# Splitting the first load of x over two DMA queues, centring the router's weights later, and 5 filler matmuls in place of 14

## What is computed

```python
def _smooth_quant_linear(x, w):
    amax_x = jnp.max(jnp.abs(x), axis=0)          # maximum of each column
    amax_w = jnp.max(jnp.abs(w), axis=0)
    s = jnp.sqrt(jnp.maximum(amax_x, EPS) / jnp.maximum(amax_w, EPS))
    xs, ws = x / s, w * s
    x_scale = jnp.max(jnp.abs(xs), axis=-1, keepdims=True) / QMAX
    w_scale = jnp.max(jnp.abs(ws), axis=-1, keepdims=True) / QMAX
    return round(xs / x_scale) @ round(ws / w_scale).T * x_scale * w_scale.T

h = _smooth_quant_linear(layernorm(x), w1)         # first block
x = x + _smooth_quant_linear(silu(gate(h)) * up(h), w2)

xn = layernorm(x)                                  # second block
scores = xn @ router_w                             # 512 x 8
# the two best of 8 experts for each token, weighted by a softmax over the two
x = x + sum over the two of weight * (silu(xn @ gate_e) * (xn @ up_e)) @ down_e
```

## Time and profile before

| | |
|---|---|
| median of 3 runs | 396.64 us (395.88 to 397.59) |
| the profiled execution, its own time | 398.95 us |
| its span | 397.2 us |
| PE busy | 330.9 us (83%) |
| DVE busy | 223.2 us (56%) |
| ACT busy | 206.7 us (52%) |
| POOL busy | 244.7 us (62%) |
| mean granted TensorE clock | 0.948 |

### The profile page before, as it was taken

How to read it: one execution, slowest core, us unless ns; L and a number is a source line. 1 busy time by engine, 2 the same in 40 slices (tenths; PEclk the granted TensorE clock), 3 DMA queues, 4 the chain that set the end, 5 groups by cost and what they waited for, 6 DMA issues and landing times.

```text
span 397.2 us, 6211 instructions
## 1 busy us (share of the span) xinstructions
PE 330.9 (83%) x1824; PEld 198.9 (50%) x1850; DVE 223.2 (56%) x511; ACT 206.7 (52%) x386; POOL 244.7 (62%) x271
## 2 busy tenths in 40 slices
PE   5856857858887977689889896999999999999950
PEld 3434525536665953385564453555555555545520
DVE  3575886888889958877586832333333333333310
ACT  1549838968997596128544233444444444444430
POOL 6494696889999851584471262556666676656350
PEclk9999998998999598888998999999999999999996
DMA  7772907654693417045344444556677757655542
GB/s 230 233 306 88 318 21 238 216 178 136 227 320 113 161 53 266 26 159 167 152 132 162 54 130 67 104 103 117 121 130 132 131 106 116 129 86 109 87 65 26
DMA packets 27550, 56.77 MB, mean 143 GB/s; under 512 B 2624, under 2 KB 13888, under 8 KB 25600
## 3 DMA queue, kind: packets, MB, share of 16 engines
q0 software_dynamic: 8736, 20.45, 28.4%
q1 hardware_dynamic: 18256, 35.92, 26.2%
q10 hardware_dynamic: 528, 0.02, 0.1%
HBM read 37.50 MB, written 18.87 MB: 142 GB/s over the span
## 4 chain that ended last, share of the span: by engine, by line
PE 63%; DVE 15%; POOL 10%; ACT 5%; issue 4%; DVEq 0%; ACTq 0%; POOLq 0%
PE bank_h L1299 26%; PE bank_q L1320 13%; PE bank_t L1284 5%; PE bank_q L1166 4%; DVE amax L716 4%; PE bank_q L1217 4%; DVE rmax L746 3%; POOL x L638 2%; PE bank_r L1310 2%; PE bank_h L1194 2%; PE bank_r L1255 2%; DVE xn L758 2%; DVE packed L869 2%; PE bank_t L1143 2%; PE bank_r L1175 1%
## 5 line engine op out<-in xcount | busy, mean ns | idle before, releaser
L1299 PE MATMUL bank_h<-gu_hi,xT 128*128 x312 | 105.5, 384 | 2.6 <-DVE xT L952 1.9
L952 DVE SCALAR_TENSOR_TENSOR xT<-bank_t,xT 128x512 f16<-128x512 f32 x39 | 26.8, 689 | 55.1 <-ACT xT L1082 44.4
L1320 PE MATMUL bank_q<-dn_hi,aT 128*128 x156 | 52.6, 379 | 3.5 <-DVE aT L970 2.9
L1299 PE MATMUL bank_h<-gu_lo,xT 128*128 x144 | 54.9, 381 | 0.0
L1299 PEld LDWEIGHTS bank_h<-gu_hi,xT 128*128 128x128 f16 x312 | 31.0, 99 | 32.2 <-issue 4.0
L656 POOL DMA_INDIRECT w_in<-tokens,gather_at x30 | 29.9, 998 | 22.6 <-PE bank_t L1284 10.4
L574 POOL TENSOR_TENSOR gu_lo<-stage,gu_hi 128x1024 bf16<-128x1024 f32 x16 | 34.0, 2135 | 13.7 <-ACT gu_hi L1039 13.5
L677 POOL DMA_INDIRECT out<-h,scatter_at x17 | 26.9, 1581 | 13.8 <-ACT h L1111 6.9
L1089 ACT ACTIVATE gated<-bank_h 128x256 f32<-128x256 f32 x39 | 15.0, 385 | 38.6 <-PE bank_h L1299 36.1
L716 DVE TENSOR_REDUCE amax<-bank_t 128x1 f32<-128x512 f32 x48 | 30.8, 683 | 6.1 <-PE bank_t L1155 3.3
L960 DVE SCALAR_TENSOR_TENSOR gated<-bank_h,gated 128x256 f32<-128x256 f32 x39 | 16.5, 424 | 31.1 <-ACT gated L1089 29.1
(11 more groups left out here) (194 smaller groups left out, 729.4 us busy)
## 6 DMA issues: line engine op xcount, KB each, us to landing
stage<-in_L_ffn_gate_proj SPq DMA_DIRECT2D x8, 512.0 KB, 4.3
stage<-in_L_ffn_up_proj SPq DMA_DIRECT2D x8, 512.0 KB, 5.9
stage<-in_L_ffn_down_proj SPq DMA_DIRECT2D x8, 512.0 KB, 4.5
x<-in_x SPq DMA_DIRECT2D x4, 1024.0 KB, 6.8
out<-x SPq DMA_DIRECT2D x4, 1024.0 KB, 5.0
tokens<-xn SPq DMA_DIRECT2D x4, 1024.0 KB, 5.1
x_in<-in_x SPq DMA_DIRECT2D x3, 1024.0 KB, 5.7
w_in<-in_fside_BxS2xS SPq DMA_DIRECT2D x3, 1024.0 KB, 5.4
```

Source lines behind the costliest of these rows:

```text
L952: dve.scalar_tensor_tensor(out=xT[i % 2][:, 1].rearrange("p c t -> p (c t)"), in0=bank, scalar=X_SCALE, in1=xT[i % 2][:, 0].rearrange("p c ...
L1299: ins = pe.matmul(bank, xT[i % 2][:, part, c], rhs[:, cols], start=(c == 0 and m == 0), stop=(c == C - 1 and m == 2))
L1320: ins = pe.matmul(bank, aT[i % 2][:, part, c], rhs[:, cols], start=(c == 0 and n == 0), stop=(c == FC - 1 and n == 2))
```

## The change

Three edits, all on batch 0 or on the router's weights.

1. Of the four pieces of x, SP issues 0 and 2, and ACT issues 1 and 3 as its first two instructions, ahead of `rw`.
2. The subtraction `rwc` leaves the head of DVE's program and becomes a step "centre 0" behind "x columns 0". Its wait on the means goes with it. The other wait there, on seven small constants ("floors"), goes to the first column maximum.
3. Ahead of "w1 columns 0" PE runs 5 filler matmuls in place of 14.

```diff
@@ DVE_ORDER
-    "moments 1 0, w1 columns 0, x columns 0, smoothing 1 0, smooth x 0, x scales 0, w1 scales 0, moments 1 1, "
+    "moments 1 0, w1 columns 0, x columns 0, centre 0, smoothing 1 0, smooth x 0, x scales 0, w1 scales 0, moments 1 1, "
@@ FILLERS
-    ("w1 columns", 0): 14, ("x columns", 0): 4, ("rows 1", 0): 5, ("w1 scale row", 0): 18, ("rows 1", 1): 3,
+    ("w1 columns", 0): 5, ("x columns", 0): 4, ("rows 1", 0): 5, ("w1 scale row", 0): 18, ("rows 1", 1): 3,
@@ load_x
-                    for j in range(J):
+                    for j in range(0, J, 2):
                         sp.dma_start(x_in[:, j], x_dram[b][:, j]).then_inc(sem(f"x_piece{j}"), 16)
@@ block.vector
-            dve.wait_ge(sem("floors"), 7)
-
-            dve.wait_ge(sem("means"), 1)
-            dve.tensor_tensor(rwc[:], rw[:], spread(bank_h[:, 1, 0:E], [P, C, E], 1), ALU.subtract).then_inc(sem("centred"), 1)
+            def centre(_):
+
+                dve.wait_ge(sem("means"), 1)
+                dve.tensor_tensor(rwc[:], rw[:], spread(bank_h[:, 1, 0:E], [P, C, E], 1), ALU.subtract).then_inc(sem("centred"), 1)
@@ column_max
+                if b == 0:
+                    dve.wait_ge(sem("floors"), 7)
@@ block.scalar
+            for j in range(1, J, 2):
+                act.dma_start(x_in[:, j], x_dram[0][:, j]).then_inc(sem(f"x_piece{j}"), 16)
             act.dma_start(rw[:], router_w.rearrange("(c p) e -> p c e", p=P)).then_inc(sem("router_in"), 16)
```

More of the change, by code:

```diff
@@ L973, in _ @@
             in_turn(dve_order,
-                    {"choose": choose, "place": place, "table": add_to_table, "list": list_tiles, **({"done": tiles_done} if EARLY else {}),
+                    {"centre": centre, "choose": choose, "place": place, "table": add_to_table, "list": list_tiles, **({"done": tiles_done} if EARLY else {}),
                      "indices": indices, "x low": x_low, "up": up, "a low": a_low,
```

## The result

| | before | changed |
|---|---|---|
| median of 13 runs each | 397.63 us | 401.13 us |
| ratio, 95% interval | | 1.0076 [1.005, 1.0101] |
| span of the profiled execution | 397.2 us | 399.7 us |
| its own time | 398.95 us | 401.4 us |
| mean granted TensorE clock | 0.948 | 0.948 |

The change makes the kernel slower by 0.76%, that is by 3.0 us (2.0 to 4.0), where +1.0 was forecast; 401.13 lies above the range. The ratio is that of the means, 400.71 and 397.69; the medians differ by 3.5 us. The profiled spans differ by 2.5 us.

A forecast was written before the change was run, and what follows sets the result against it. PE's queue, waiting for the router's weights, was taken to bound the start of x's columns. Late weights less fillers (+0.4 us) and the clock (+0.6), put on the median 396.64, gave 397.6 us, range 394.8 to 399.8.

The forecast's parts named there:

- The x path: x's landing, DVE's statistics and ACT's normalising up to `xn`: forecast to gain 0.75 us, `xn` ready at 14.0.
- the other bound of 6.9: Landing of x's last piece if always 5.6 us behind its issue; the gain would then be 1.7 us.
- The path that decides: PE's queue behind `rw` sets the start of x's columns, at 16.6 us; `xn` waits 2.6 us for them.
- R: Landing of `rw`, third on ACT's queue: 8.2 us, the middle of 7.8 and 8.6, 3.6 us later than before.
- The clock: Some of w1's transposes on PE run at the low clock level: +0.6 us, between 0 and +0.9.
- The other terms: On PE's path, means take 1.85 us and 5 fillers 2.15 against 5.35 for 14, giving 3.2 us back.
- Rival B: PE's clock stays low from the means through x's columns: +2.9 us together, 399.5 us, slower; chance 0.15.
- The base: Time before that the shift was added to: 396.64 us, the median of the runs shown.
- rival A: `rw` is not held up, landing at 5.45, and x's landing decides: -1.6 us, 395.0 us; chance 0.27.
- The shift is handed on: A shift in the start of x's columns on PE goes through to the kernel's end at its full size.

The follow-up runs named there:

- e8: Changed kernel with PE's means behind x's columns, the subtraction behind the root's reciprocal, and fillers 10, 7 and 2; ratio to before 0.9986.
- e9: e8 with all four pieces of x on SP's queue; ratio to before 0.9999.
- e10: e8 with 5 fillers ahead of the rows in place of 2; ratio to before 0.9927.
- e11: e10 with all four pieces of x on SP's queue; ratio to before 0.9946.
- e5: Kernel before with only the pieces of x split over two queues; ratio to before 1.0105.
- e2: Changed kernel with 14 fillers ahead of w1's columns in place of 5; ratio to before 1.0128.
- e3: Kernel before with only the fillers ahead of w1's columns cut from 14 to 5; ratio to before 0.9987.
- e4: Kernel before with only the subtraction moved behind x's columns; ratio to before 0.9995.
- e6: Changed kernel without any filler ahead of w1's columns; ratio to before 1.0017.
- e1: Changed kernel with ACT issuing the router's weights ahead of its two pieces of x; ratio to before 1.0014.

## Why the prediction was wrong

**The x path gained more than forecast.** The statistics were to end at 8.5 with the landings unchanged, and ended at 8.19; `xn` was to be ready at 14.0, and was at 13.68. SP's and ACT's issues cost nothing, and the subtraction took 0.18 us where DVE waits for the root. But the landings did change: the last piece came at 7.0, near the other bound of 6.9. I had taken it that the bytes set them, not the issue. In the six profiles with two queues in this order it lands at 6.9 to 7.2, in the five with one queue at 7.4 to 8.2. Little of this reaches `xn`, since DVE takes the last two pieces back to back: e8 has `xn` 0.40 us ahead of e9, and e10 0.31 ahead of e11.

The Trainium skill, "DMA: Bandwidth & Descriptors", "Issuing engines are not separate DMA queues", says that issuing from several engines saves only the time to issue. The trace agrees as far as it goes: the last piece was issued 0.93 us earlier and landed 0.8 us earlier. It did not follow from this, as the prediction has it, that the landing stays. The runs do not separate the saved issue from a second cause, that the packets of `rw` no longer stand beside those of x.

**The path that decides was right**: PE's queue behind the landing of `rw`, with `xn` waiting for PE. e5, e2, e8 and the change itself all show it.

**R was mis-sized: 9.13 in place of 8.2, by 0.9 us.** I took the middle of 7.8 (the landing of x's last piece) and 8.6 (the 2.1 us that `rw` had taken on fresh queues, put behind x). The upper bound, w1's first half at 9.35, was the better row, though not for its reason: in the change that half landed at 8.7, ahead of `rw`. The changed kernel's queues of SP (q1) and ACT (q10), from 6.5 to 7 and from 7 to 7.5 us:

```profile
q1 hardware_dynamic: 161, 0.16, 88.9%
q10 hardware_dynamic: 143, 0.01, 17.8%
...
q1 hardware_dynamic: 146, 0.15, 89.8%
q10 hardware_dynamic: 148, 0.00, 16.5%
```

Before, 231 and 205 packets went in half a microsecond each, with gaps; now they come at 143 and 148, beside w1's packets on SP's queue, and it takes from about 6.2 to 8.5 us to move them. The Trainium skill, "DMA: Bandwidth & Descriptors", "Queues, rings and completion order", says that a DMA engine goes round its queues packet by packet, and consumes descriptors in ring order. The trace agrees: both queues move packets in the same half microseconds, and those of `rw` begin when the last of x's on their own queue are through, near 6 us, which no run had shown before. By that rule R was "anywhere from 7.8 to 9.35"; I should have put more weight on the far end, since by then both queues are full.

**The clock was mis-sized: +1.0 in place of +0.6.** All 16 transposes ran at the low level, which was the upper bound. The price read from the earlier trace rows for that was 0.9; it measured 1.02.

**The other terms held.** Means +4.56, fillers 5.35 - 2.15 = -3.2, w1's columns +1.02, the 4 fillers -0.07: +2.3, which is 17.91 less 15.61. I had +1.0. Rival B had this mechanism and the right size (+2.9), but with the low level reaching through the fillers and x's columns, which it did not do (x's maxima took as long as before), and with R at 8.2. What happened is the forecast's own chain with both uncertain terms near the upper end, R just short of it and the clock just above it; my own range for the forecast ended at +1.7 because it took R up to 8.6 only.

**The base was low by 1.0 us.** The forecast of 397.6 stands on 396.64, the median of three runs; the median of 13 is 397.63. Of the 3.5 us between 397.6 and 401.13, 1.0 is this and not the mechanism. The 0.7 us between +2.3 at x's columns and +3.0 measured lie within the interval.

One reading under rival A was off too: by 4.6, when `rw` had landed, 0.61 MB of x's 1.05 had moved, so more than half. It bears on no term of the sum.

**The shift is handed on**, as assumed. Over the kernels of the table the root's start and the measured ratio go together: +4.4 and +4.7 us in e5 and e2 are 4.2 and 5.1 us measured, and +2.4 is 3.0 in the change (each of these to 1 us or more either way). Below about 1 us the profile of a single execution does not order the kernels: e3 starts its root 1.1 us late and e4 0.6, and neither is slower. The starts of the experts' tiles compare even less: the profiled executions of e4 and e6 had a mean granted clock of 0.959, that of before 0.948, and both start them 2.1 us earlier than before although their roots start later.

## What to carry to other kernels

Before a small load is moved back in a queue, ask who stands behind it: here 16 KB whose product is needed some 100 us later held up PE's whole program, because their first user was PE's first instruction. An early start for the large load gains nothing while that is so; moving the user, with the fillers fitted again, gained 0.7% (e10) and 0.5% with the loads left where they were (e11), while moving the loads alone (e5) cost 1.05%. When an engine's start shifts, its fillers have to be fitted again at every wait nearby, not only at the one that moved: with 3 fillers too few, half of a lead of 1.7 us was gone in the profile of e8.

## What the runs showed of the hardware

- The 512 small packets of `rw` (16 KB) land 3.8 us after their issue at the head of a queue (3.6 to 4.8 in six profiles with `rw` first or alone on ACT's queue), and 7.4 to 7.7 us when they stand behind two pieces of 256 KB and beside w1 on the other queue.
- They also hold up what is behind them: in e1 a piece of x behind `rw` took up to 7.3 us to land, against 5.8 in the change.
- x's last piece landed at 6.9 to 7.2 with x on two queues ahead of `rw` (six profiles), and at 7.4 to 8.2 with x on SP's queue alone (five).
- The landing of `rw` with the same DMAs as before varied by 1.2 us between profiles (4.4 in e9 and e11, 4.6 in before and e4, 5.6 in e3). I had taken it as fixed.
- With the start of PE 4.6 us later, the first rise of TensorE's clock also came later: between 10.6 and 11.3 us before, after 16.5 in the change and near 15 in e2 and e6. The start alone does not set it: e1 starts PE at 5.11 and its transposes of w1 are all at the low level, the rise coming near 15.3, while in e3, with a start at 5.73, it came by 10.4, and in e8, whose ten fillers run from 4.55 without a gap, by 8.8.
- Executions of the same kernel differ in their mean granted clock, and in time with it: 22 of before on one chip take 396.9 us in the mean at 0.95 or more (4 of them) and 399.2 below (18).
